# Turned x from the input for five groups, scores summed in PSUM, gate and up loaded without copies

## The reference

```python
def _layernorm(x, eps=1e-05):
    return (x - mean(x)) / sqrt(var(x) + eps)

def xattn(x, k, v, Wh, wg_w, wo_w, gn_gamma, gn_beta):
    Q, K, V = heads of x, k, v times Wh[h]                 # 4 heads of 128
    scores = einsum('bshe,bthe->bhst', Q, K) / sqrt(hd)
    A = maximum(abs((scores * Dn).sum(axis=0)), 1.0)       # summed over the batch
    O = einsum('hst,bthe->bshe', A, V)
    Y = (O - mu) / sqrt(var + GN_EPS) * gn_gamma + gn_beta
    return relu(x @ wg_w) * Y @ wo_w

x = x + tanh(g_xattn) * xattn(_layernorm(x), ctx, ctx, ...)
x = x + tanh(g_ffn) * ffn(_layernorm(x), ...)              # (silu(x gate' * gs) * (x up' * us)) down' * ds
```

## Time and profile before

| | us |
|---|---|
| three runs | 1504.81, 1507.49, 1509.27 (median 1507.49) |
| profiled execution, its own time | 1504.33 |
| its span | 1502.5 |
| TensorE busy in the span | 1483.4 |
| granted clock of TensorE, mean | 0.999 |
| groups 3 to 7 of the first stage, each | 21.20 |

### The profile page before, as it was taken

The page is one execution under the profiler, slowest core; times in us unless marked ns, Lnnn a source line. Parts: engine busy times, 40 slices in busy tenths (PEclk is TensorE's granted clock), DMA queues, the critical chain, the costliest instruction groups (busy, mean ns, idle before and its releaser), DMA issues.

```text
span 1502.5 us, 20476 instructions
## 1 busy us (share of the span) xinstructions
PE 1483.4 (99%) x7182; PEld 1246.3 (83%) x7182; DVE 1096.5 (73%) x1592; ACT 698.3 (46%) x1094; POOL 744.9 (50%) x774
## 2 busy tenths in 40 slices
PE   7999999999999999999999999999999999999998
PEld 5888888888888887888888888888888888888887
DVE  7776778788578687677686763777778778778672
ACT  4444434445565545555646534344344344443442
POOL 5556666771445553545645534137237137237236
PEclk9999999999999999999999999999999999999999
DMA  6888788876778779888898785373473562562422
GB/s 225 301 262 271 262 282 282 255 234 221 250 229 279 237 221 305 261 246 282 240 288 281 209 240 158 116 217 105 125 212 107 144 208 95 146 199 93 149 90 85
DMA packets 237753, 316.05 MB, mean 210 GB/s; under 512 B 135696, under 2 KB 161680, under 8 KB 237456
## 3 DMA queue, kind: packets, MB, share of 16 engines
q1 hardware_dynamic: 237648, 314.71, 66.0%
HBM read 210.32 MB, written 117.31 MB: 218 GB/s over the span
## 4 chain that ended last, share of the span: by engine, by line
PE 86%; DVE 4%; DMA 3%; POOL 2%; SPq 1%; ACT 1%; issue 1%; DVEq 0%; ACTq 0%; POOLq 0%
PE ps L1785 33%; PE po L1785 10%; PE pyb L1664 8%; PE ptb L1785 7%; PE pyb L1785 7%; PE ps L1699 5%; PE po L1664 5%; PE pyb L1769 3%; PE ptb L1769 3%; PE pyb L1773 2%; PE ptb L1773 1%; PE ptb L1669 1%; PE ps L1664 1%; DMA wy_scratch<-misc 1%; POOL reg L1536 1%
## 5 line engine op out<-in xcount | busy, mean ns | idle before, releaser
L1785 PE MATMUL ps<-op,wbuf 128*128 128x512 f32 x880 | 217.3, 389 | 0.0
L1563 POOL TENSOR_TENSOR p5b<-p5b,p1b 128x512 f32<-128x512 f32 x55 | 71.3, 1296 | 268.6 <-ACT p5b L797 268.6
L1491 POOL TENSOR_SCALAR rs<-mv 128x1 f32<-128x1 f32 (+1 forms) x132 | 48.4, 367 | 295.7 <-DVE mv L1116 157.3
L1785 PEld LDWEIGHTS ps<-op,wbuf 128*128 128x128 f32 x880 | 165.2, 188 | 34.3
L1574 POOL TENSOR_TENSOR hsp<-hall,hsp 128x640 fp32r<-128x640 f32 (+2 forms) x90 | 172.3, 1931 | 42.3 <-ACT hsp L824 42.3
L1664 PE MATMUL pyb<-reg,xreg 128*128 128x512 f32 x708 | 177.9, 398 | 2.2 <-DVE reg L1005 2.2
L1785 PE MATMUL po<-op,wbuf 128*128 128x512 f32 x660 | 168.3, 389 | 0.0
L1664 PEld LDWEIGHTS pyb<-reg,xreg 128*128 128x128 f32 x708 | 129.8, 189 | 28.4 <-DVE reg L1005 2.4
L1785 PEld LDWEIGHTS po<-op,wbuf 128*128 128x128 f32 x660 | 123.9, 188 | 25.7
L1785 PE MATMUL ps<-reg,gate 128*128 128x512 f32 x528 | 130.8, 390 | 0.0
L1785 PE MATMUL ps<-reg,up 128*128 128x512 f32 x528 | 130.7, 390 | 0.0
(11 more groups left out here) (154 smaller groups left out, 2937.7 us busy)
## 6 DMA issues: line engine op xcount, KB each, us to landing
wbuf<-ws_scratch SPq DMA_DIRECT2D x55, 896.0 KB, 4.7
xr<-in_x SPq DMA_DIRECT2D x62, 512.0 KB, 5.4
raw<-in_ctx_t SPq DMA_DIRECT2D x32, 512.0 KB, 4.6
w_scratch<-tmp SPq DMA_DIRECT2D x64, 256.0 KB, 5.1
v_scratch<-tmp SPq DMA_DIRECT2D x64, 256.0 KB, 4.5
raw<-v_scratch SPq DMA_DIRECT2D x32, 512.0 KB, 6.5
x_scratch<-xr SPq DMA_DIRECT2D x32, 512.0 KB, 5.6
xr<-x_scratch SPq DMA_DIRECT2D x32, 512.0 KB, 5.8
```

The source lines that it names most:

```text
L1491: e.tensor_scalar(dst, var, eps, None, ALU.add).then_inc(s["eps"])
L1563: e.tensor_tensor(p5b[n % 2][:, :], p5b[n % 2][:, :], p1b[n % 2][:, :], ALU.add).then_inc(s["p15"])
L1785: last = e.matmul(dst, l, r, start=(k == 0 and i == 0), stop=(k == n - 1 and i == 1), skip_group_check=sums)
```

## The change

Three things.

1. **Turned x.** The host passes x also as [512, 8192] (`in_x_t`). For groups 4 to 8 (`LAID`, 20 tiles) TensorE doesn't transpose. x is still loaded in rows and DVE still takes its statistics, but their mean and reciprocal deviation are computed for four tiles in one go (`rstd_rows`), stored as two rows of 512 numbers in DRAM (`row_store`) and loaded into all 128 partitions (`row_load`). The turned x of the group is loaded into `xts` (`xt_load`, two DMAs); POOL subtracts the row of means (`x_centre`), DVE multiplies by the row of deviations (`x_scale`), ACT writes the high part (`x_hi`) and DVE the low part (`x_lo`), one k (512 columns) at a time. While group g runs, this is the work for group g+1, so it lies in groups 3 to 7.
2. **Scores in PSUM.** The v matmuls no longer start a new sum: both score regions gather all tiles. The V region must be zeroed by ACT after each `v_out` (`vz`, 62 times), DVE clears both tensors at the start, and `v_acc` (64 times) goes. At the end DVE adds the two regions.
3. **Weights.** The eight parts of gate and up are loaded straight from the inputs, by POOL's DMA queue; their copies in DRAM go. The copies of down stay. The low-bits checks follow another table (`LOWS`), in part a group later. In DVE's loop, `see(k)` takes statistics of the group's list until k are left (in a laid group two at first, then one each time), and `check(k)` does the low-bits checks of the weights in the same way.

The diff, cut to what matters:

```diff
+LAID = range(4, 9)
+LOWS = {2: 2, 3: 1, 4: 1, 5: 2, 6: 2, 7: 2, 8: 2, 9: 2, 10: 2, 11: 2, 12: 2, 13: 2, 14: 2}
+def by_tensor(t):
+    return sum(i // 4 not in LAID for i in range(t))
+def stats_until(g):
+    return min(4 * g + (14 if g + 2 in LAID else 12 if g + 3 in LAID else 10), B)
...
+        xts = [over("xts0", "gate", 16.5, [128, 2, 512]), over("xts1", "up", 16.5, [128, 2, 512])]
+        rowsb = [over("rowsb0", "up", 5.5, [128, 2, 512]), over("rowsb1", "turned1", 0, [128, 2, 512])]
...
+            def row_store(i):
+                p.wait_ge("rsg", i + 1)
+                at = 4 * LAID[i] % 8
+                for row, src in enumerate((mv[:, at:at + 4, 0], rs[:, at:at + 4])):
+                    e.dma_start(rows_s[i, row].rearrange("(t p) -> p t", p=128), src, allow_slow_non_contiguous=True).then_inc(s["sto"], 16)
+            def row_load(i):
+                p.wait_ge("sto", 32 * (i + 1))
+                if i >= 2:
+                    p.wait_ge("xsc", 4 * i - 4)
+                e.dma_start(rowsb[i % 2][:, :, :].rearrange("p a n -> p (a n)"),
+                            rows_s[i].rearrange("a n -> (a n)").partition_broadcast(128)).then_inc(s["bc"], 16)
+            def xt_load(i, half):
+                if i:
+                    p.wait_ge("tbxe", 4 * LAID[i - 1] + 2 * half + 2)
+                cols = slice(512 * LAID[i], 512 * LAID[i] + 512)
+                e.dma_start(xts[half][:, :, :], xt_v[:, 2 * half:2 * half + 2, cols]).then_inc(s[f"xtl{half}"], 16)
...
+            def x_hi(i, k):
+                p.wait_ge("xsc", 4 * i + k + 1)
+                p.wait_ge("w", 4 * LAID[i] - 4)
+                e.copy(xnt[LAID[i] % 2][0][:, k, :], x_part(k)).then_inc(s["xth"])
             def v_out(t):
...
                 e.copy(tmp[:, 2 + t % 2, :].rearrange("p (h n) -> p h n", h=4), ps[t % 2][:, :, 0, :]).then_inc(s["vev"])
+                if t + 2 < B:
+                    p.wait_ge("vev", t + 1)
+                    p.wait_ge("ones", 4)
+                    e.copy(ps[t % 2][:, :, 0, :], nil[:, 0:1].to_broadcast([128, 4, 128])).then_inc(s["vz"])
...
+            def x_scale(i, k):
+                p.wait_ge("xc", 4 * i + k + 1)
+                e.tensor_tensor(x_part(k), x_part(k), rowsb[i % 2][:, 1, :], ALU.mult).then_inc(s["xsc"])
+            def x_lo(i, k):
+                p.wait_ge("xth", 4 * i + k + 1)
+                hi, lo = [q[:, k, :] for q in xnt[LAID[i] % 2]]
+                e.tensor_tensor(lo, x_part(k), f(hi), ALU.subtract).then_inc(s["tbxe"])
-            def v_acc(t):
-                p.wait_ge("vev", t + 1)
...
-                    e.tensor_tensor(acc, acc, ps[t % 2][:, :, 1, :], ALU.add).then_inc(s["acc"])
...
+            e.memset(ps[0][:, :, :, :], 0).then_inc(s["clear"])
             stats(0)
...
             xt_lo(2)
             wg_lo(0)
+            p.wait_ge("tbxe", 3)
+            e.memset(ps[1][:, :, :, :], 0).then_inc(s["clear"])
             xt_lo(3)
...
                 z_lo(4 * g + 2)
                 z_lo(4 * g + 3)
+                if laid:
+                    see(max(count - step * at_once, 0))
+                    x_scale(i, 0)
...
+                see(max(count - step * at_once, 0))
+                if laid:
+                    x_scale(i, 1)
+                    x_lo(i, 0)
...
+                if laid:
+                    x_scale(i, 2)
+                    x_lo(i, 1)
+                else:
+                    xt_lo(n + 1)
+                    norm(n + 2)
+                see(max(count - step * (at_once + 1), 0))
+                if laid:
+                    x_scale(i, 3)
+                    x_lo(i, 2)
...
+                check(1)
                 if g in (7, 8, 9, 10, 12, 13, 14):
...
+                see(max(count - step * (at_once + 2), 0))
+                if laid:
+                    x_lo(i, 3)
...
+                see(0)
+                check(0)
...
+            def rstd_rows(i):
+                t = 4 * LAID[i]
+                p.wait_ge("mv", t + 4)
+                power(rs[:, t % 8:t % 8 + 4], mv[:, t % 8:t % 8 + 4, 1], 1e-5, "rsg")
+            def x_centre(i, k):
+                p.wait_ge("bc", 16 * (i + 1))
+                p.wait_ge(f"xtl{k // 2}", 16 * (i + 1))
+                e.tensor_tensor(x_part(k), x_part(k), rowsb[i % 2][:, 0, :], ALU.subtract).then_inc(s["xc"])
+            def weights_load(n):
...
+                src, dst = chunks[n]
+                e.dma_start(dst, src.bitcast(f32r)).then_inc(s[f"wld{n % 2}"], 16)
...
             for g in range(NG - 1):
+                for chunk in {1: (0,), 2: (1,), 3: (2,), 4: (3,), 6: (4,), 8: (5, 6), 9: (7,)}.get(g, ()):
+                    weights_load(chunk)
                 ct_split(g + 1, 0)
+                if laid:
+                    x_centre(i, 0)
+                    x_centre(i, 1)
...
+                if laid_next:
+                    rstd_rows(g + 2 - LAID[0])
+                if laid:
+                    x_centre(i, 2)
                 ct_split(g + 1, 1)
+                if laid:
+                    x_centre(i, 3)
                 ct_split(g + 1, 2)
...
                 if t >= 2:
-                    p.wait_ge("vev", t - 1)
-                    p.wait_ge("acc", t - 1)
+                    p.wait_ge("vz", t - 1)
+                else:
+                    p.wait_ge("clear", t + 1)
-                                        wh_and_z(q, h, b), start=(n == 0), stop=(n == 2))
+                                        wh_and_z(q, h, b), start=False, stop=(n == 2), skip_group_check=True)
...
+                turning = more and g + 1 not in LAID
...
+                if turning:
                     xt(n)
```

More of the change, by code:

```diff
@@ L39, in wait_ge, with x_until, lows_before @@
             self.engine.wait_ge(self.s[name], value)
+def by_tensor(t):
+    return sum(i // 4 not in LAID for i in range(t))
+def stats_until(g):
+    return min(4 * g + (14 if g + 2 in LAID else 12 if g + 3 in LAID else 10), B)
+def x_until(g, late):
+    return min(2 * g + late + (7 if g + 3 in LAID or (g + 2 in LAID and not late) else 6), B // 2)
+def lows_before(g):
+    return sum(LOWS.get(i, 0) for i in range(g))
 def ctl(g, h):
@@ L208, in gated_layer @@
         ct_v = ctx_t.rearrange("(h p) n -> p h n", p=128)
+        xt_v = x_t.rearrange("(k p) n -> p k n", p=128)
         down_flat = down_t.rearrange("(p a) n -> p (a n)", p=128)
         wo_v = wo.rearrange("(k p) n -> p k n", p=128)
[L211 to L215, removed]
+        chunks = [(src[128 * k:128 * k + 128, :], dst[:, k, :])
+                  for first in range(2)
+                  for src, dst in ((gate_t, gate), (up_t, up))
+                  for k in (first, first + 2)]
         def hall_tile(i, first, end):
@@ L503, in _ @@
             ct_load(2, 0)
+            for q in range(6, x_until(0, 1)):
+                x_load(q)
             e.dma_start(colsb[:, :], cols).then_inc(s["cols"], 16)
@@ L875, in _ @@
                 z_hi(4 * g + 3)
-                if more:
+                if not more:
+                    v_hi(0)
+                elif not laid:
                     xt_hi(n)
-                else:
-                    v_hi(0)
                 v_out(4 * g)
+                if laid:
+                    x_hi(i, 0)
                 v_out(4 * g + 1)
@@ L1041, in low_weights @@
                     p.wait_ge(f"wld{c % 2}", 16 * (c // 2 + 1))
-                    low_bits(chunks[c][2][:, 704 * half:704 * half + 704], "and")
+                    low_bits(chunks[c][1][:, 704 * half:704 * half + 704], "and")
                 else:
@@ L1301, in _, with see, check @@
             xt_lo(7)
-            v_acc(2)
             norm(8)
             stats(9)
-            v_acc(3)
             for g in range(1, NG):
-                n, more = 4 * g + 4, g + 1 < NG
+                n, more, i = 4 * g + 4, g + 1 < NG, g + 1 - LAID[0]
+                laid = g + 1 in LAID
+                to_see = list(range(stats_until(g - 1), stats_until(g)))
+                count, step = len(to_see), 2 if len(to_see) > 4 else 1
+                at_once = 2 if g + 2 in LAID else 1
+                checks_here = list(range(lows_before(g), lows_before(g + 1)))
+                def see(left):
+                    while len(to_see) > left:
+                        stats(to_see.pop(0))
+                def check(left):
+                    while len(checks_here) > left:
+                        low_weights(*divmod(checks_here.pop(0), 2))
                 z_lo(4 * g)
                 z_lo(4 * g + 1)
-                if more:
+                if more and not laid:
                     norm(n + 1)
@@ L1611, in _ @@
                     weight_sums(2 * g - (10 if g < 9 else 12))
[L1612 removed]
+                if n + 5 < B and not laid_next:
                     rstd(n + 5)
```

205 lines of the change are left out of this document (110 added, 95 removed).

## The result

The changed kernel takes 1554.16 us (median of four runs, 1553.0 to 1555.23), beside 1506.15 for the kernel before (four runs, 1503.87 to 1509.27): 1.0327 times as long, with an interval of 1.0312 to 1.0342. That is 48 us slower by the medians and 49 by the ratio, where 5 us faster was forecast and the slowest rival said 7 us slower. The profiled execution took 1555.23 us, its span is 1553.4, 50.9 above that of before.

A forecast was written before the change was run, and what follows sets the result against it. TensorE, busy 1483.4 of 1502.5 us, was taken as the bound. Terms 8.8 - 1.5 - 3.5 + 2.0 - 0.7 gave 5.1 us less: 1507.49 to 1502.4 us, range 1496 to 1510.

The forecast's parts named there:

- the slowest rival: Laid groups: POOL sets the pace, delayed by DVE's operations; 7.2 us slower, 1514.7; chance 0.16 with slower DMA.
- The transposes: TensorE in groups 3 to 7: 20 tiles lose four transposes each, 8.8 us gained, 1.76 a group.
- The wait behind the z's: Between z and v in laid groups: TensorE waits 0.3 us for z_lo, 1.5 lost in five groups; bounds 0 and 2.8.
- DMA and SP: Transfers and SP's queue: bytes about even, a group's two row stores take SP about 1.3 us; cost 0.
- the size of the seam: Between laid groups: late x_lo holds up z, 0.4 or 0.9 us a group, 3.5 lost; bounds 0.5 and 7.5.
- POOL holds, with little left: POOL in laid groups: 18.1 us of work in 19.4 for groups 5 to 7, ctx splits in time for v.
- The late row: Row or turned x landing late would act through x_centre's wait; counted with the slowest rival, no separate size.
- The loads by POOL's queue: Eight weight loads on POOL: 1 us each, cost nothing, or 2 us in group 8 if the spare is gone.
- The gaps of groups 8 to 14: Gaps of 4.0 us: 2.75 us less DVE work a group gives back 2.0; bounds 4.0 gained, 1.5 lost.
- The start: Before the first w: DVE's second clearing delays xt_lo(3), 0.7 us lost; bounds 0 and 1.2.
- The end of the stage and the second stage: Last additions as many in a row as before, and the second stage: 0 for each.

The follow-up runs named there:

- e12: e9 also without rstd_rows, row stores and row loads, so x of the laid groups goes in as it comes; 1511.86 us, ratio 1.0049.
- e9: e1 without x_centre and x_scale in the laid groups, so turned x is split as loaded; 1516.45 us, ratio 1.0073.
- e1: The changed kernel with each row of statistics stored as 128 pieces of 16 bytes instead of 512 of 4; 1534.7 us, ratio 1.02.
- after: The changed kernel itself, with all three parts, against the kernel before; 1554.16 us, ratio 1.0327.
- e11: The kernel before plus ten row stores of zeros in 512 four-byte pieces, read by nobody, in groups 2 to 6; 1523.94 us, ratio 1.0125.
- e3: The changed kernel with no laid group: scores in PSUM and the weights' loads only; 1516.87 us, ratio 1.0079.
- e10: e3 with the eight gate and up loads spread one to each of POOL's iterations 0 to 7; 1510.59 us, ratio 1.0035.
- e2: The kernel before with only the scores summed in PSUM: clearings, 62 zeroings on ACT, no v_acc; 1510.62 us, ratio 1.0033.
- e8: e1 without x_scale, DVE's four multiplications in a laid group; 1519.75 us, ratio 1.0095.
- e6: The kernel before with gate and up loaded straight from inputs by POOL's queue, one part in each iteration 0 to 7; 1504.3 us, ratio 0.9996.
- e13: e11 with each store of zeros as 128 pieces of 16 bytes instead of 512 of four; 1503.3 us, ratio 0.9993.

## Why the prediction was wrong

The account in us, each from a pair of kernels above:

| term | forecast | measured | from |
|---|---|---|---|
| transposes less the wait behind z | 7.3 gained | 7.75 gained | e12, 5 x 1.55 |
| seam, x_lo alone | in the next | 4.5 lost | e12's laid groups |
| rows of 16-byte pieces, rstd_rows | 0 | 4.6 lost | e9 - e12 |
| x_centre and x_scale | 3.5 lost at the seam | 18.3 lost | e1 - e9 |
| row stores of 4-byte pieces | 0 | 19.5 lost | after - e1; e11 |
| pair of loads in POOL's queue | 0 | 6.3 lost | e3 - e10 |
| part 2: start, groups 8 to 14, later | 1.3 gained | 5.9 lost | e2 |

They add up to 51.4 lost, beside 1504.7 for the kernel before on the chip of the experiments; the 49.5 measured against that are 1.9 less, mainly since e12 stands 5.0 below e3 and not 3.25 as its laid groups would have it: its group 8 is 2.6 shorter as well. Each row is a term's price in its own pair of kernels. The terms overlap, as the pair of loads shows, and the order in which they are taken out decides how the sum is shared.

*The transposes* were right in mechanism and size. In e12 the one group without a wait for x_lo is 19.65 us long; 19.44 + 0.3 was forecast. *The wait behind the z's* is 0.9 us in five groups of e12, 0.2 each, beside the 0.3.

*The first step that failed is in "DMA and SP"*: "a group's two take about 1.3, and nothing needs that V slot for several us. Cost 0". SP's time was right (1.05 us in e11). But the sentence priced only the issue on SP, and not the 1024 packets behind it. In e11's window of the stores, w's and V's stores and the loads of x and ctx land after 9.0 to 12.5 us instead of 2.9 to 5.0. The paragraph goes on, "if DMAs got slower, v_out would wait", which is what happened, for w_out above all, and gives it no price. Nothing in the earlier trace rows had a piece under 128 bytes, so this was a cost that no row of before shows; it needed an upper bound and got none. A loss of 19.5 us is by itself enough to leave the range. That e11 loses as much as e1 gives back doesn't say that both lose it in the same way: the changed kernel's chain goes through the row's landing and `row_load`, e11's through w's stores.

*The second is the size of the seam*, "I put 0.4 us a group for groups 3 and 4 ... and 0.9 for 5 to 7: 3.5 us in all", with an upper bound of 7.5. The kind of delay was right: x_lo and the checks, with two inputs in SBUF, against POOL. The size was not. The bound let one instruction be late by one POOL subtraction. But each k goes through x_centre on POOL, x_scale on DVE, x_hi on ACT and x_lo on DVE, each waiting for the one before, four times a group. e1 loses 18.3 us by x_centre and x_scale where the step had 3.5; 8 of the 18.4 us in its laid groups come with x_scale alone, and 12 with the two together.

*A term that the forecast doesn't have* is TensorE's clock. It took TensorE's own time as fixed, and only added waits. The changed kernel's five laid groups take 42.6 us more than e12's (145.3 and 102.75); 32.5 of it is idle time, and for 10.1 TensorE is busy longer with the same matmuls, at a mean granted clock of 0.88 to 0.94. e1, with waits of up to 4.5 us, has 0.87 to 0.93 in four of its five, and 21.6 to 22.7 us busy there instead of 19.9 in e12.

*POOL.* "POOL holds, with little left" was too easy: 18.1 us was forecast for groups 5 to 7, and 19.0, 21.2 and 19.6 were measured, of which only the first would have fitted into a group of 19.4. The slower rival, that POOL's amount sets the pace, is still not what made these groups as long as they are, as e8 shows; the cause it named, that DVE's operations and POOL's hold each other up, has a part in the 18 us. The late row, put aside as "counted with this one", is a cause of its own: its stores cost 19.5, and e11 loses as much with nobody waiting for the row.

*The loads by POOL's queue*: "they stand in front of ctx splits with 4 us to spare, so they cost nothing, and 2 us in group 8 if that spare is gone". One load costs 0.65 and nothing on the path (e6, e10). Two in one iteration cost 6.3 in e3, because the second starts 7 us after the first. The step priced each issue and not the distance of two. The second starts when the first has landed; why, the trace doesn't show. That the wait goes when the loads are an iteration apart is shown.

*The gaps of groups 8 to 14*: "2.75 us less DVE work a group should give back about half, 2.0". It gave nothing. DVE's work fell and the stalls stayed. In the one group looked at, group 14 of e2, which lost 1.9, TensorE waits for a norm, xt_lo and z_lo on DVE, and DVE for ACT, to which the change added 62 x 0.588 us of zeroing (0.6 was forecast). That the others are the same isn't shown.

*The start* lost 1.24 at the first w (15.34 instead of 14.10), the forecast's upper bound of 1.2 and not its 0.7; the start of group 1 moves by as much as 1.2 from one kernel to another with the same start, so what of it reaches the end is open.

*The end of the stage and the second stage*: forecast 0. From group 15 on after takes 4.2 us more, e2 3.0; e11, which changes nothing there, 3.2. That this belongs to the change isn't shown.

No kernel here beats the one before. The best that keeps a part of the change is e6, which is no faster. By an estimate from the rows above, e8 with its pair of loads apart would come to some 1513 (1519.75 - 6.3), and it doesn't normalise x rightly. What would be left to try is a laid group whose statistics reach TensorE without DVE and POOL meeting on the same x.

## What to carry to other kernels

Price a small transposing store by its packets and not by its bytes or its issue: put it into the kernel before, with nobody reading it, and look at what its neighbours in the queue take. A row of operations that goes to and fro between VectorE and GpSimd on SBUF tiles can lose time at every link, so bound it by the number of links and not by one. Count what a wait does to TensorE's clock with the wait. And where an instruction is removed from the engine with room, ask first whether the stalls go through that engine at all.

## What the runs showed of the hardware

- Two stores of 512 pieces of four bytes, 4 KB together, held the 16 DMA engines at under 100 GB/s for 6.7 us and moved the landing of a 256 KB store from 2.9 to 12.5 us (e11); the same bytes in 256 pieces of 16 bytes (two stores of 128) landed in 4.6 us (e13) and moved nothing that a run of 1504 us can tell.
- A second load of 704 KB by POOL's queue, right behind the first, left POOL idle for 6.5 to 8.9 us and started 0.3 us after the first had landed (e3, the changed kernel, e8, e9, e12); loads 17 to 24 us apart took 0.65 to 0.79 each (e6).
- In a stop of 5.8 us TensorE's granted clock fell to 0.50 (1.2 GHz), and the twelve matmuls behind it took 4.58 us instead of 2.91 (the changed kernel, at 157.47 and 163.31); over groups with such stops its mean was 0.87 to 0.94 instead of 1.00.
- A VectorE check with both inputs in SBUF that began inside a GpSimd sum of 2.3 us took 2.53 us instead of 0.88 (the changed kernel, four times).
- Zeroing 512 numbers a partition in PSUM takes ACT 0.588 us, as long as a copy out of it; clearing 1024 takes DVE 0.91.
